# Key and query parts by batch, part and component in memory; a stack in two halves of eight heads

## The chip, the cores and the metric

The kernel runs on one core of one Trainium2 chip. The time is the device time in microseconds of one execution. The core has TensorE (PE, with its weight loads as PEld), VectorE (DVE), ScalarE (ACT), GpSimd (POOL) and SyncE (SP, here the queue that issues nearly all DMAs); 16 DMA engines move the data. Two per cent of the time is 9.9 us.

## What is computed

Two layers, each a cross-attention block and a mixture of experts, over x of shape (8, 128, 256). The first block is a long convolution of products of the context; the second, which the change concerns, is an attention with 16 heads of 8 components. Cut to that part:

```python
q = proj(Wq, bq, query).reshape(b, HD, H, n)          # b = 8, HD = 8, H = 16, n = 256
k = proj(Wk, bk, key).reshape(b, HD, H, n)            # key and value come from the context
q, k = (rotary(encoding, t) for t in (q, k))
scores = jnp.einsum('bdhn,bdhm->bhnm', q, k) / np.float32(np.sqrt(HD))
prob = jax.nn.softmax(scores, axis=-1)
x = jnp.einsum('bhnm,bdhm->bdhn', prob, v)
out = jnp.einsum('oi,bin->bon', Wm, x.reshape(b, d_model, n)) + bm[None, :, None]
...
x = x + jnp.tanh(g_xattn[1]) * _L1_xattn_ref(_layernorm(x, axis=-1), ctx_2048, ctx_2048, ...)
```

## The kernel before

The program is written out by hand, one instruction stream per engine, ordered by semaphores. It goes through the convolution (to about 84 us), the first experts (16 pairs of experts, to about 212 us, then the sum of their outputs in L1033 and L1038 to 282 us), the attention (about 258 to 410 us, its first row maxima between the expert sums), and the second experts (to the end). A pair of batches is a chunk `c`, of which there are four.

**Parts.** Keys and queries are float32; each is split into three bfloat16 parts. A product of two float32 numbers is the sum over part pairs, so a head's score is one matmul over 72 rows: 3 x 3 part pairs times 8 components. The rotated keys of a chunk are in `KR["a"]`, its parts in `KR["parts"]` (queries: `QR`); ACT casts parts 0 and 1 (`cast`, L591), POOL (keys, L430) or DVE (queries, L1309 to L1318) subtracts.

**Memory.** The layout must change: parts lie with component and head on partitions and position along the row, while a matmul needs components on partitions and one head at a time. So SP writes them to memory: keys at L316 during the convolution, once a chunk (`kp_out`), queries in `qout(c)` (L357, L358), once a chunk (`qp_out[c]`). Queries are written with five part rows, parts 0, 1, 2, 0, 1, so that three shifted windows can be read. Before ACT overwrites the parts of a chunk it waits for the write of the chunk before.

**Stacks.** `stack(b)` (L343) loads the key stack `KST[b % 4]` and the query stack `QST[b % 4]` of batch b, 72 rows of 16 heads times 256 positions each: for each of three groups of 24 rows one DMA for keys and one for queries, six in all, on one semaphore `st_in[b % 4]`. It waits until batch b - 4 has been used (`st_pe`), or until POOL has filled rows of ones (`kst_one`, L548). `maxrow(b)` (L351) adds three rows to the query stack with the negative row maxima.

**Order on PE.** `smax(H)` (L1007) multiplies the scores of head H (of 128 over all batches) for DVE's row maximum (`rowmax`, L1457); twenty of them run early, between the expert sums. In the attention loop group G = 8b + g computes `scores(G)` for two heads with the maximum rows (L1065, exponential on ACT, L708), `values` (L1080), and two more `smax` (three in the first four groups). At g = 4 stands `maxturn(b + 1)` (L1022), after the first `smax` of batch b + 2; DVE's `maxcopy` (L1478) then releases `maxrow(b + 1)` on SP. `smax` waits once a batch, at head 0, for the six DMAs of the stack.

**Order on SP** in this part: `qout(0)`, a wait for all key parts and query chunk 0, `stack(0)`, `stack(1)`, `qout(1)`, `qout(2)`, `maxrow(0)`, `stack(2)`; then for each b `maxrow(b + 1)`, `stack(b + 3)`, and for b = 0 `qout(3)`.

`P` = 128, `L` = 256, `NH` = 16, `HD` = 8, `NT` = 72, `UN` = 8, `NST` = 4, `QC` = 4, `B` = 8.

Of the kernel before, what the change touches and what calls it, by code (L numbers as in the profile page):

```python
# [22 lines left out]
BF16 = mybir.dt.bfloat16  # L23
# [6 lines left out]
B, S, L = 8, 128, 256  # L30
P = 128
# [20 lines left out]
TOP, LOW = B * HH * HD, B * HH * HH  # L52
HALF = TOP + LOW
NST = 4


def build(nc, x, ctx_in, g_xattn, g_ffn, ssm, dskip, gate_w, wgu, wdn, wsgu, wsdn, enc,
          wq, bq, wk, bk, wv, bv, wm, bm, rw, wa, wb, out):
    es = ExitStack()
    with es:  # L60
# [6 lines left out]

        kpad_d = nc.dram_tensor("kpad_d", [NH, P + L], F32, kind="Internal")
        rows_d = nc.dram_tensor("rows_d", [T + 1, L], F32, kind="Internal")
        kparts_d = nc.dram_tensor("kparts_d", [3, P, T * 2], BF16, kind="Internal")  # L70
        qparts_d = nc.dram_tensor("qparts_d", [5, P, T * 2], BF16, kind="Internal")


        X = sb("X", [P, B, L])
# [57 lines left out]
        OL = r2(14336, 2048, "p (k c) -> p k c", k=LB * B)  # L132

        def rope_views(base):
            return dict(a=base[:, 0:512], b=base[:, 512:1024],
                        parts=base[:, 1024:1792].bitcast(BF16).rearrange("p (s n) -> p s n", s=3))
        KR = rope_views(SA[:, :, :].rearrange("p s n -> p (s n)")[:, 0:1024 + 768])
        EB = SA[:, 2, 0:512].rearrange("p (k f c) -> p k f c", k=LB, f=2)

# [115 lines left out]
        mo_pe, mo_x = sem("mo_pe"), sem("mo_x")  # L255
        qp_pe, qp_free, qp_parts = sem("qp_pe"), sem("qp_free"), sem("qp_parts")
        qp_out = [sem(f"qp_out{c}") for c in range(B // 2)]
        st_in = [sem(f"st_in{s}") for s in range(NST)]
        kst_one = sem("kst_one")
        s_pe, s_max, ms_ok, mt_pe, mr_ok = (sem(n) for n in ("s_pe", "s_max", "ms_ok", "mt_pe", "mr_ok"))  # L260
        mrow_in, st_pe, p_ok, pv_pe = (sem(n) for n in ("mrow_in", "st_pe", "p_ok", "pv_pe"))
# [20 lines left out]
        @block.sync  # L282
        def _(sp):
            sp.dma_start(KPAD[:, P:P + L], ssm).then_inc(ld_ssm, 16)
            sp.dma_start(DSK[:, :], dskip.rearrange("(h a) -> h a", a=1)).then_inc(ld_ssm, 16)
            sp.dma_start(CTX[:, :, :], ctx_in.rearrange("b s l -> s b l")).then_inc(ld_ctx, 16)
            sp.dma_start(X[:, :, :], x.rearrange("b s l -> s b l")).then_inc(ld_x, 16)

            sp.wait_ge(kpad_ok, 1)
            sp.dma_start(kpad_d.ap(), KPAD).then_inc(kpad_out, 16)  # L290
            sp.wait_ge(kpad_out, 16)

            tap = bass.AP(tensor=kpad_d, offset=1, ap=[[1, P], [P + L, NH], [1, L]])
            sp.dma_start(TT, tap).then_inc(ld_tt, 16)
            sp.wait_ge(ld_w, 16 * 14)

            def load_up(k):
                sp.dma_start(WG[:, 2 * (k % NPAIR):2 * (k % NPAIR) + 2, :, :],
                             wgu[2 * k:2 * k + 2].rearrange("e (k p) f -> p e k f", p=P))\
                  .then_inc(ld_up[k % NPAIR], 16)  # L300

            def load_down(k):
                sp.dma_start(WD[0:HI, 2 * (k % NPAIR):2 * (k % NPAIR) + 2, :, :],
                             wdn[2 * k:2 * k + 2].rearrange("e (k p) n -> p e k n", p=HI))\
                  .then_inc(ld_down[k % NPAIR], 16)

            for k in range(NPAIR):
                load_up(k)
                load_down(k)
            sp.dma_start(SHW[:, :, :], wsgu.rearrange("(k p) f -> p k f", p=P)).then_inc(ld_sh, 16)  # L310
            sp.dma_start(SHD[:, 0:2, :], wsdn[0:256, :].rearrange("(k p) n -> p k n", p=P)).then_inc(ld_sh, 16)
            sp.dma_start(SHD[0:96, 2, :], wsdn[256:352, :]).then_inc(ld_sh, 16)

            for c in range(QC):
                sp.wait_ge(kp_parts, c + 1)
                sp.dma_start(kparts_d.ap().rearrange("s p n -> p s n")[:, :, c * 512:c * 512 + 512],  # L316
                             KR["parts"]).then_inc(kp_out, 16)

            sp.wait_ge(ln_ok, LN3)
            sp.dma_start(rows_d.ap()[1:T + 1, :].rearrange("(b s) l -> s b l", b=B), XN[:, :, :])\  # L320
              .then_inc(rows_out, 16)

            for k in range(NPAIR, KT0 + 1):
                if k < KT0:
                    sp.wait_ge(gu_pe, k - NPAIR + 1)
                    load_up(k)
                if k > NPAIR:
                    sp.wait_ge(y_pe, k - NPAIR)
                    load_down(k - 1)

            sp.wait_ge(y_pe, KT0)
            sp.dma_start(WA, wa.rearrange("e (k p) r -> p e k r", p=P)).then_inc(ld_ab, 16)
            sp.dma_start(WB, wb.rearrange("e p n -> p e n")).then_inc(ld_ab, 16)
            def stack(b):

                if b >= NST:
                    sp.wait_ge(st_pe, UN * (b - NST + 1))
                else:
                    sp.wait_ge(kst_one, b + 1)
                for r in range(3):  # L340
                    rows = slice(3 * HD * r, 3 * HD * r + 3 * HD)
                    for dst, src, part in ((KST, kparts_d, 0), (QST, qparts_d, r)):
                        sp.dma_start(dst[b % NST][rows, :, :],  # L343
                                     src.ap()[part:part + 3].rearrange("s (d h) (b n) -> (s d) h b n", h=NH, b=B)[:, :, b, :])\
                          .then_inc(st_in[b % NST], 16)

            def maxrow(b):

                sp.wait_ge(mr_ok, b + 1)
                for s in range(3):  # L350
                    sp.dma_start(QST[b % NST][NT + s:NT + s + 1, :, :].rearrange("p h (m n) -> p (h m) n", m=LB),  # L351
                                 MR[32 * s:32 * s + 32, :]).then_inc(mrow_in, 16)

            def qout(c):
                sp.wait_ge(qp_parts, c + 1)
                cols = slice(c * 512, c * 512 + 512)
                sp.dma_start(qparts_d.ap().rearrange("s p n -> p s n")[:, 0:3, cols], QR["parts"]).then_inc(qp_out[c], 16)  # L357
                sp.dma_start(qparts_d.ap().rearrange("s p n -> p s n")[:, 3:5, cols], QR["parts"][:, 0:2, :])\  # L358
                  .then_inc(qp_out[c], 16)

            qout(0)
            sp.wait_ge(kp_out, 16 * QC)
            sp.wait_ge(qp_out[0], 32)
            stack(0)
            stack(1)
            qout(1)
            qout(2)
            maxrow(0)
            sp.wait_ge(qp_out[1], 32)
            stack(2)  # L370
            for b in range(B):
                if b + 1 < B:
                    maxrow(b + 1)
                if b + 3 < B:
                    sp.wait_ge(qp_out[(b + 3) // 2], 32)
                    stack(b + 3)
                if b == 0:
                    qout(QC - 1)

            for c in range(2):  # L380
                sp.wait_ge(o_ok, 2 * c + 2)
                sp.dma_start(out.rearrange("b s l -> s b l")[:, 4 * c:4 * c + 4, :], X[:, 4 * c:4 * c + 4, :])\
                  .then_inc(out_dma, 16)
            sp.wait_ge(out_dma, 32)
            sp.wait_ge(zrow_out, 16)
# [3 lines left out]
        def _(pool):  # L389
# [93 lines left out]
                root(2 * c, 2 * c + 2)  # L483


            pool.wait_ge(kp_out, 16 * QC)
            def shared(u):
                n2, f = divmod(u, 3)
                m = SHF[f][1]
# [73 lines left out]
        def _(act):  # L563
# [19 lines left out]
            def cast(parts, a, c, s, q):  # L583

                if c >= 1 and s == 0:
                    act.wait_ge(qp_out[c - 1] if q else kp_out, 32 if q else 16 * c)
                if q:
                    act.wait_ge(cast_in, 2 * c + s + 1)
                else:
                    act.wait_ge(k_rest if s else k_sum, c + 1)  # L590
                act.activation(parts[:, s, :], a, ACT.Copy).then_inc(cast_out, 1)  # L591
# [193 lines left out]
        def _(pe):  # L785
# [211 lines left out]
            def smax(H):  # L997

                b, h = divmod(H, NH)
                if H == 0:  # L1000
                    pe.wait_ge(qp_free, 2)
                if h == 0:
                    pe.wait_ge(st_in[b % NST], 16 * 6 * (b // NST + 1))
                if H >= 2:
                    pe.wait_ge(s_max, H - 1)
                for m in range(LB):
# [231 lines left out]
        def _(dve):  # L1238
# [55 lines left out]
            def rope(c, R, bias, sem_pe, sem_free, sem_parts, cast0, b0):  # L1294

                def turn_up():
                    dve.wait_ge(sem_pe, c + 1)
                    if c >= 1:
                        dve.wait_ge(sem_parts, c)
                    dve.scalar_tensor_tensor(out=two(R["a"]), in0=two(PS[:, b0, :]), scalar=BT[:, bias:bias + 1],  # L1300
                                             in1=bc(FQ[:, 0, :], [P, 2, L], 1), op0=ALU.add, op1=ALU.mult)
                    dve.scalar_tensor_tensor(out=two(R["b"]), in0=two(PS[:, b0 + 1, :]),
                                             scalar=BT[:, bias + 1:bias + 2],
                                             in1=bc(FQ[:, 1, :], [P, 2, L], 1), op0=ALU.add, op1=ALU.mult)\
                        .then_inc(sem_free, 1)
# [218 lines left out]
            def qlast(i):  # L1524

                dve.wait_ge(qp_pe, QC + i)
                if i == 0:
                    dve.wait_ge(qp_parts, QC - 1)
                dve.scalar_tensor_tensor(out=two(QR["b" if i else "a"]), in0=two(PS[:, 7, :]),
                                         scalar=BT[:, 2 + i:3 + i], in1=bc(FQ[:, i, :], [P, 2, L], 1),  # L1530
                                         op0=ALU.add, op1=ALU.mult).then_inc(qp_free, 1)

# [135 lines left out]
```

## Time and profile before

| | |
|---|---|
| median of 3 runs | 494.24 us (487.6, 494.24, 494.79) |
| profiled execution | 491.66 us, span 489.8 us |
| granted TensorE clock, mean | 0.927 |
| PE, DVE, ACT, POOL busy | 84%, 60%, 34%, 31% of the span |

In the profile, times are microseconds from the start of the span unless marked ns. `SPq` is SP's queue: the duration of a row there is the time to issue a DMA, not to move it. A landing is when the DMA's semaphore is complete. PEclk is the share of full TensorE speed that was granted. The DMA share is the mean busy share of the 16 DMA engines. A name such as `R` can stand for several tiles of the same memory region; `kparts_d` and `qparts_d` are the tensors in memory. In brackets behind a row stands how long the engine was idle before it and what ended that.

### The profile page before, as it was taken

The page shows a single profiled execution, that of the slowest core. Times are in us where ns is not written, and L with a number is a line of the kernel's source. Part 1 is how long each engine was busy: PE and PEld are TensorE (multiplying, and loading weights), DVE is VectorE, ACT ScalarE, POOL GpSimd, SP SyncE. Part 2 cuts the span into 40 slices and gives each one's busy share as a digit, 9 for nine tenths or more (in the row PEclk, how much of TensorE's full clock was granted, in tenths as well). Part 3 has the DMA queues.
Part 4 walks back from the last instruction along what each step waited for, and adds up shares of the span by engine and source line. Part 5 has one row for each costly group of instructions (what it writes and reads, how often), then busy time and mean ns, then how long its engine had stood idle before and what let it go on. Part 6 is the DMA issues. An engine that isn't in the chain of part 4 may idle for free.

```text
span 489.8 us, 7462 instructions
## 1 busy us (share of the span) xinstructions
PE 413.6 (84%) x2821; PEld 266.0 (54%) x2821; DVE 295.0 (60%) x613; ACT 166.6 (34%) x300; POOL 153.8 (31%) x234
## 2 busy tenths in 40 slices
PE   1489993869769768699998768999999989899996
PEld 1378883824535435368886534455555545465554
DVE  1859997499916454633447778688898823322212
ACT  1221320133345434200110125467767785311110
POOL 0658898248972210502111060022112231110000
PEclk9999996588859998999999869699999999899999
DMA  6692010200049999741183141543345000000101
GB/s 197 190 286 87 33 34 32 87 0 0 1 121 267 254 258 233 188 143 36 58 162 83 57 97 34 119 87 75 64 78 98 3 3 1 1 0 1 43 0 43
DMA packets 49867, 43.53 MB, mean 89 GB/s; under 512 B 4101, under 2 KB 48553, under 8 KB 49833
## 3 DMA queue, kind: packets, MB, share of 16 engines
q1 hardware_dynamic: 47264, 40.65, 32.8%
q0 software_dynamic: 800, 2.10, 1.5%
q10 hardware_dynamic: 1768, 0.33, 0.4%
q8 instruction: 22, 0.36, 0.3%
q14 instruction: 13, 0.10, 0.1%
HBM read 36.55 MB, written 6.32 MB: 88 GB/s over the span
## 4 chain that ended last, share of the span: by engine, by line
PE 50%; DMA 16%; POOL 13%; DVE 11%; issue 3%; SPq 3%; ACT 3%; DVEq 0%; POOLq 0%; ACTq 0%
DMA WG<-in_L_ffn_w_gate_up_dram 10%; PE PS L1038 8%; PE PS L1221 7%; PE PS L1184 6%; PE PS L1080 5%; PE PS L1007 5%; PE PS L1065 4%; PE PS L957 3%; DMA R<-qparts_d 3%; DMA X<-in_x_dram 2%; DVE MX L1457 2%; PE PS L1033 2%; POOL SA L430 2%; POOL R L491 2%; SPq L343 2%
## 5 line engine op out<-in xcount | busy, mean ns | idle before, releaser
L1457 DVE TENSOR_REDUCE MX<-PS 128x2 f32<-128x512 f32 x128 | 85.9, 709 | 18.4 <-PE PS L1007 18.0
L708 ACT ACTIVATE R<-PS 128x1024 f32<-128x1024 f32 x64 | 65.4, 1024 | 46.9 <-PE PS L1065 46.5
L1038 PE MATMUL PS<-R 128*128 128x256 bf16 x384 | 47.3, 276 | 0.0
L1007 PE MATMUL PS<-R 72*128 72x256 bf16 x192 | 39.9, 295 | 6.6 <-DVE MX L1457 5.5
L1080 PE MATMUL PS<-R 128*32 128x256 f32 x512 | 42.6, 407 | 1.4 <-ACT R L718 1.0
L1038 PEld LDWEIGHTS PS<-R 128*128 128x128 bf16 x384 | 37.9, 99 | 5.9
L411 POOL TENSOR_TENSOR RSB<-RSA,MH 128x2 f32<-128x2 f32 (+2 forms) x20 | 14.3, 713 | 75.9 <-issue 40.2
L553 POOL TENSOR_TENSOR X<-X,R 128x256 f32<-128x256 f32 x8 | 5.8, 727 | 99.9 <-ACT R L731 99.9
L957 PE MATMUL PS<-WG,R 128*64 128x352 f32 x128 | 24.0, 496 | 14.8 <-DMA WG<-in_L_ffn_w_gate_up_dram 14.2
L1221 PE MATMUL PS<-WG,R 128*128 128x256 f32 x128 | 33.1, 405 | 1.3 <-DVE R L1624 1.2
L1065 PE MATMUL PS<-R 75*128 75x256 bf16 x192 | 31.6, 290 | 1.7 <-DMA R<-MR 1.7
L1624 DVE TENSOR_TENSOR R<-PS,R 128x512 f32<-128x512 f32 x16 | 11.0, 690 | 35.5 <-ACT R L775 35.5
L1007 PEld LDWEIGHTS PS<-R 72*128 72x128 bf16 x192 | 15.0, 103 | 29.0 <-DVE MX L1457 16.4
L1184 PE MATMUL PS<-CTX,WG 128*128 128x512 f32 x64 | 30.3, 595 | 0.0
L1221 PEld LDWEIGHTS PS<-WG,R 128*128 128x128 f32 x128 | 24.2, 198 | 7.7 <-issue 2.9
L518 POOL DMA_INDIRECT R<-rows_d,IX x16 | 15.4, 962 | 32.2 <-PE PS L947 30.4
L591 ACT ACTIVATE WD<-WD 128x512 bf16<-128x512 f32 x8 | 5.0, 628 | 58.9 <-DVE WD L1309 56.6
L1267 DVE TENSOR_SCALAR XN<-X,MV,RS 128x256 f32<-128x256 f32 x32 | 15.7, 525 | 14.8 <-POOL RS L415 14.8
L775 ACT ACTIVATE R<-PS 128x512 f32<-128x512 f32 x16 | 9.4, 597 | 43.1 <-PE PS L1197 39.8
L904 PE MATMUL PS<-CTX,SHW 128*128 128x512 f32 (+1 forms) x48 | 23.9, 661 | 0.0
L1065 PEld LDWEIGHTS PS<-R 75*128 75x128 bf16 x192 | 19.5, 104 | 7.7 <-DMA R<-MR 2.4
L957 PEld LDWEIGHTS PS<-WG,R 128*64 128x64 f32 x128 | 9.4, 145 | 25.7 <-issue 21.7
(237 smaller groups left out, 796.2 us busy)
## 6 DMA issues: line engine op xcount, KB each, us to landing
WG<-in_L_ffn_w_gate_up_dram SPq DMA_DIRECT2D x16, 704.0 KB, 12.6
WD<-in_L_ffn_w_down_dram SPq DMA_DIRECT2D x16, 352.0 KB
R<-kparts_d SPq DMA_DIRECT2D x24, 192.0 KB
R<-qparts_d SPq DMA_DIRECT2D x18, 192.0 KB
R<-kpad_d SPq DMA_DIRECT2D x1, 2048.0 KB, 7.9
kparts_d<-SA SPq DMA_DIRECT2D x4, 384.0 KB, 2.5
qparts_d<-WD SPq DMA_DIRECT2D x4, 384.0 KB, 3.2
SA<-qparts_d SPq DMA_DIRECT2D x6, 192.0 KB
```

The source lines that it names most:

```text
L518: pool.indirect_dma_start(XG[:, k % 4, :], None, rows_d.ap(), bass.IndirectOffsetOnAxis(ap=IX[:, k:k + 1], axis=0))\
L708: act.activation(PX[:, G % 4].rearrange("p h m n -> p (h m n)"), PS[:, 2 * (G % 2):2 * (G % 2) + 2, :].rearrange("p a n -> p (a n)"), ACT. ...
L904: last = pe.matmul(PS[0:m, 2 + 2 * (u % 2) + half, :], SHW[:, k, half * SH + f0:half * SH + f0 + m], XNT[:, k, n2 * 512:n2 * 512 + 512], s ...
L957: last = pe.matmul(PS[eo * SLOTC:eo * SLOTC + SLOTC, 2 + k % 2, 0:2 * INTER], XB[:, k % 2, j, eo * SLOTC:eo * SLOTC + SLOTC], WG[:, (2 * k ...
L1007: last = pe.matmul(PS[:, 4 + H % 2, m * L:m * L + L], QST[b % NST][0:NT, h, m * P:m * P + P], KST[b % NST][0:NT, h, :], start=True, stop=True)
L1038: last = pe.matmul(o, OHT[:, k, b * P:b * P + P], Y[:, k, s, :], start=False, stop=(k == KT0 - 1 and s == 2))
L1065: last = pe.matmul(PS[:, 2 * (G % 2) + hh, m * L:m * L + L], KST[b % NST][0:SROWS, 2 * g + hh, m * P:m * P + P], QST[b % NST][0:SROWS, 2 * ...
L1080: last = pe.matmul(PS[32 * j:32 * j + 32, 6, 0:L], V32[:, b % 2, m, 4 * q + j, :], PX[:, (2 * Q + j // 2) % 4, j % 2, m, :], start=(m == 0 ...
L1184: last = pe.matmul(PS[:, 4 + u % 2, :], WA[:, e, k, :], XNT[:, k, c * 512:c * 512 + 512], start=(k == 0), stop=(k == 1))
L1221: last = pe.matmul(PS[:, 2 * c + t // 2, (t % 2) * L:(t % 2) * L + L], AE[:, u % 2, t * P:t * P + P], WB[:, e, :], start=(e == 0 and t % 2 ...
L1267: ins = dve.tensor_scalar(XN[:, b, :], X[:, b, :], MV[:, b, 0:1], RS[:, b:b + 1], ALU.subtract, ALU.mult)
L1457: dve.tensor_reduce(MX[:, H % NH, :], PS[:, 4 + H % 2, :].rearrange("p (m n) -> p m n", m=LB), AX, ALU.max).then_inc(s_max, 1)
```

## The change

The tensors in memory are laid out by batch, part, component and head: `[B, 5, P, L]` for keys and `[B, 3, P, L]` for queries, so that one batch's part and component is a run of 16 heads times 256 positions (8 KB). The five part rows are now the keys', and the queries have three; the set of part pairs is the same. In SBUF the parts of a chunk are laid out by batch first. Keys of a chunk are written by four DMAs, queries by one. A stack is loaded by four DMAs (keys and queries, each in two halves of eight heads) of 72 rows of 4 KB each, whose source pattern has three leading entries: for keys with a step of one part, for queries with step 0. Each half has a semaphore, and `smax` waits for it at heads 0 and 8. DVE's rotary instructions take views of the same elements.

```diff
-        kparts_d = nc.dram_tensor("kparts_d", [3, P, T * 2], BF16, kind="Internal")
-        qparts_d = nc.dram_tensor("qparts_d", [5, P, T * 2], BF16, kind="Internal")
+        kparts_d = nc.dram_tensor("kparts_d", [B, 5, P, L], BF16, kind="Internal")
+        qparts_d = nc.dram_tensor("qparts_d", [B, 3, P, L], BF16, kind="Internal")
...
         def rope_views(base):
-            return dict(a=base[:, 0:512], b=base[:, 512:1024],
-                        parts=base[:, 1024:1792].bitcast(BF16).rearrange("p (s n) -> p s n", s=3))
+            flat = base[:, 1024:1792].bitcast(BF16)
+            return dict(a=base[:, 0:512].rearrange("p (b n) -> p b n", b=2),
+                        b=base[:, 512:1024].rearrange("p (b n) -> p b n", b=2),
+                        parts=flat.rearrange("p (b s n) -> p s b n", b=2, s=3),
+                        rows=flat.rearrange("p (r n) -> p r n", n=L))
...
-        st_in = [sem(f"st_in{s}") for s in range(NST)]
+        st_in = [[sem(f"st_in{f}_{s}") for s in range(NST)] for f in range(2)]
...
                 sp.wait_ge(kp_parts, c + 1)
-                sp.dma_start(kparts_d.ap().rearrange("s p n -> p s n")[:, :, c * 512:c * 512 + 512],
-                             KR["parts"]).then_inc(kp_out, 16)
+                for i in range(2):
+                    to = kparts_d.ap()[2 * c + i].rearrange("s p n -> p s n")
+                    sp.dma_start(to[:, 0:3, :], KR["rows"][:, 3 * i:3 * i + 3, :]).then_inc(kp_out, 16)
+                    sp.dma_start(to[:, 3:5, :], KR["rows"][:, 3 * i:3 * i + 2, :]).then_inc(kp_out, 16)
...
-                for r in range(3):
-                    rows = slice(3 * HD * r, 3 * HD * r + 3 * HD)
-                    for dst, src, part in ((KST, kparts_d, 0), (QST, qparts_d, r)):
-                        sp.dma_start(dst[b % NST][rows, :, :],
-                                     src.ap()[part:part + 3].rearrange("s (d h) (b n) -> (s d) h b n", h=NH, b=B)[:, :, b, :])\
-                          .then_inc(st_in[b % NST], 16)
+                for dst, src, parts, step in ((KST, kparts_d, 5, HD * ROW), (QST, qparts_d, 3, 0)):
+                    for f in range(2):
+                        rows = bass.AP(tensor=src, offset=b * parts * HD * ROW + f * (ROW // 2),
+                                       ap=[[step, 3], [ROW, 3 * HD], [1, ROW // 2]])
+                        sp.dma_start(dst[b % NST][0:NT, f * UN:f * UN + UN, :].rearrange("p h n -> p (h n)"), rows)\
+                          .then_inc(st_in[f][b % NST], 16)
...
             def qout(c):
                 sp.wait_ge(qp_parts, c + 1)
-                cols = slice(c * 512, c * 512 + 512)
-                sp.dma_start(qparts_d.ap().rearrange("s p n -> p s n")[:, 0:3, cols], QR["parts"]).then_inc(qp_out[c], 16)
-                sp.dma_start(qparts_d.ap().rearrange("s p n -> p s n")[:, 3:5, cols], QR["parts"][:, 0:2, :])\
+                sp.dma_start(qparts_d.ap()[2 * c:2 * c + 2].rearrange("b s p n -> p (b s) n"), QR["rows"])\
                   .then_inc(qp_out[c], 16)
...
-                if h == 0:
-                    pe.wait_ge(st_in[b % NST], 16 * 6 * (b // NST + 1))
+                if h % UN == 0:
+                    pe.wait_ge(st_in[h // UN][b % NST], 16 * 2 * (b // NST + 1))
```

`ROW` is `NH * L` = 4096 elements. The waits on `kp_out` count 64 a chunk and those on `qp_out[c]` count 16, as many as the DMAs now give.

## Rows read from the trace of the kernel before

**Rows 1.** The page: busy time, the 40 slices, the DMA queues.
```profile
PE 413.6 (84%) x2821; PEld 266.0 (54%) x2821; DVE 295.0 (60%) x613; ACT 166.6 (34%) x300; POOL 153.8 (31%) x234
...
q0 software_dynamic: 800, 2.10, 1.5%
```

**Rows 2.** The chain that ended last, in one turn of the batches: start, us, what.
```profile
322.44 0.84 SPq L343
...
326.61 6.31 DMA R<-qparts_d
```

**Rows 3.** Timeline of SP's queue: start us, us to issue, line, transfer.
```profile
242.94 0.93 SPq L343 DMA_DIRECT2D R<-kparts_d  x1
...
254.43 1.25 SPq L357 DMA_DIRECT2D qparts_d<-WD  x1
...
284.31 0.83 SPq L343 DMA_DIRECT2D R<-kparts_d  x1
...
302.41 0.83 SPq L343 DMA_DIRECT2D R<-kparts_d  x1
...
335.13 1.82 SPq L351 DMA_DIRECT2D SA<-MR  x3
337.06 0.82 SPq L343 DMA_DIRECT2D R<-kparts_d  x1
```

**Rows 4.** Timeline of PE: first score matmuls of batches 0, 2, 3, 4 and 7.
```profile
258.72 0.38 PE L1007 MATMUL PS<-R 72*128 72x256 bf16 x2
...
297.13 0.38 PE L1007 MATMUL PS<-R 72*128 72x256 bf16 x2
...
317.37 0.38 PE L1007 MATMUL PS<-R,SA 72*128 72x256 bf16 x2
...
332.96 0.39 PE L1007 MATMUL PS<-R 72*128 72x256 bf16 x2 [0.80 <-DMA R<-qparts_d]
...
376.56 0.38 PE L1007 MATMUL PS<-R,SA 72*128 72x256 bf16 x2
```

**Rows 5.** Busy time by stretch: us, then PE, PEld, DVE, ACT, POOL, PEclk, DMA share, GB/s.
```profile
284.00:298.00 14.00, 10.69 (x60) 4.58 (x58) 10.66 (x21) 4.12 (x5) 5.21 (x7) 0.63 0.44 85
298.00:318.00 20.00, 18.46 (x141) 9.27 (x137) 13.88 (x29) 10.20 (x15) 0.00 (x0) 0.74 0.42 94
...
333.00:347.00 14.00, 14.00 (x141) 8.17 (x142) 11.94 (x25) 9.99 (x17) 2.57 (x8) 1.00 0.44 87
...
362.30:376.50 14.20, 14.20 (x143) 8.27 (x144) 12.54 (x29) 10.61 (x17) 2.56 (x8) 1.00 0.44 86
```

**Rows 6.** The stack's line L343: who waited for it (us, times).
```profile
  PE PS L1007: 1.0, 2
```

**Rows 7.** Busy time by stretch, columns as in Rows 5: DMA share and GB/s last.
```profile
44.00:46.20 2.20, 2.20 (x13) 1.81 (x12) 2.17 (x4) 0.00 (x0) 2.20 (x5) 1.00 0.54 182
276.00:278.50 2.50, 1.81 (x15) 1.50 (x16) 1.94 (x6) 0.00 (x0) 0.00 (x0) 0.88 0.82 269
...
357.00:361.00 4.00, 4.00 (x46) 2.33 (x39) 3.78 (x8) 2.70 (x4) 0.36 (x2) 1.00 0.92 150
150.00:200.00 50.00, 38.60 (x307) 22.29 (x303) 25.64 (x66) 21.64 (x44) 8.21 (x9) 0.97 0.97 251
```

**Rows 8.** DMA issues: queue, count, KB each, median us to landing.
```profile
kparts_d<-SA SPq DMA_DIRECT2D x4, 384.0 KB, 2.5
...
R<-MR SPq DMA_DIRECT2D x18, 8.0 KB, 1.9
```

**Rows 9.** Timeline: ACT's cast that waits for qout(1), and head 16.
```profile
272.41 0.63 ACT L591 ACTIVATE WD<-WD 128x512 bf16<-128x512 f32 x1 [18.73 <-DVE WD L1309]
...
277.44 0.38 PE L1007 MATMUL PS<-R 72*128 72x256 bf16 x2
```

**Rows 10.** Timeline: key chunk 0 goes out, and the cast behind it.
```profile
43.59 0.37 SPq L316 DMA_DIRECT2D kparts_d<-SA  x1
...
49.63 0.63 ACT L591 ACTIVATE SA<-SA 128x512 bf16<-128x512 f32 x1 [8.09 <-POOL SA L424]
```

More of the change, by code:

```diff
@@ L54 @@
 NST = 4
+ROW = NH * L
 def build(nc, x, ctx_in, g_xattn, g_ffn, ssm, dskip, gate_w, wgu, wdn, wsgu, wsdn, enc,
@@ L355, in qout @@
                 sp.wait_ge(qp_parts, c + 1)
-                cols = slice(c * 512, c * 512 + 512)
-                sp.dma_start(qparts_d.ap().rearrange("s p n -> p s n")[:, 0:3, cols], QR["parts"]).then_inc(qp_out[c], 16)
-                sp.dma_start(qparts_d.ap().rearrange("s p n -> p s n")[:, 3:5, cols], QR["parts"][:, 0:2, :])\
+                sp.dma_start(qparts_d.ap()[2 * c:2 * c + 2].rearrange("b s p n -> p (b s) n"), QR["rows"])\
                   .then_inc(qp_out[c], 16)
             qout(0)
-            sp.wait_ge(kp_out, 16 * QC)
-            sp.wait_ge(qp_out[0], 32)
+            sp.wait_ge(kp_out, 64 * QC)
+            sp.wait_ge(qp_out[0], 16)
             stack(0)
@@ L368, in _ @@
             maxrow(0)
-            sp.wait_ge(qp_out[1], 32)
+            sp.wait_ge(qp_out[1], 16)
             stack(2)
@@ L374, in _ @@
                 if b + 3 < B:
-                    sp.wait_ge(qp_out[(b + 3) // 2], 32)
+                    sp.wait_ge(qp_out[(b + 3) // 2], 16)
                     stack(b + 3)
@@ L483, in _ @@
                 root(2 * c, 2 * c + 2)
-            pool.wait_ge(kp_out, 16 * QC)
+            pool.wait_ge(kp_out, 64 * QC)
             def shared(u):
@@ L585, in cast @@
                 if c >= 1 and s == 0:
-                    act.wait_ge(qp_out[c - 1] if q else kp_out, 32 if q else 16 * c)
+                    act.wait_ge(qp_out[c - 1] if q else kp_out, 16 if q else 64 * c)
                 if q:
@@ L1299, in turn_up @@
                         dve.wait_ge(sem_parts, c)
-                    dve.scalar_tensor_tensor(out=two(R["a"]), in0=two(PS[:, b0, :]), scalar=BT[:, bias:bias + 1],
+                    dve.scalar_tensor_tensor(out=R["a"], in0=two(PS[:, b0, :]), scalar=BT[:, bias:bias + 1],
                                              in1=bc(FQ[:, 0, :], [P, 2, L], 1), op0=ALU.add, op1=ALU.mult)
-                    dve.scalar_tensor_tensor(out=two(R["b"]), in0=two(PS[:, b0 + 1, :]),
+                    dve.scalar_tensor_tensor(out=R["b"], in0=two(PS[:, b0 + 1, :]),
                                              scalar=BT[:, bias + 1:bias + 2],
@@ L1528, in qlast @@
                     dve.wait_ge(qp_parts, QC - 1)
-                dve.scalar_tensor_tensor(out=two(QR["b" if i else "a"]), in0=two(PS[:, 7, :]),
+                dve.scalar_tensor_tensor(out=QR["b" if i else "a"], in0=two(PS[:, 7, :]),
                                          scalar=BT[:, 2 + i:3 + i], in1=bc(FQ[:, i, :], [P, 2, L], 1),
```

## The prediction

> **What bounds the kernel now.** I read the page's busy shares first: PE is busy 84% of the span, the next engine 60%, so PE and what it waits for set the time [rows 1]. The change touches only how key and query parts go to memory and come back, so I then followed the stretch where this matters, 243 to 377 us. The chain of waits passes in it twice through SP's queue and a stack's transfers: six issues of about 0.8 us, then 6.31 us to landing [rows 2], then PE's score matmul L1007. The SP queue shows why [rows 3]. In a steady batch one stack is issued from 322.44; PE's first L1007 on it runs at 332.96, after 0.8 us idle on the transfer [rows 4]; the maximum rows go out at 335.13 and the next stack at 337.06. These steps are a loop: on PE the transposition L1022 (which maxrow needs) stands behind the first L1007 of the next stack, and stack(b+3) stands behind maxrow(b+1) on SP. One turn is 10.5 us of stack (322.44 to 332.96) and 4.1 us of the rest (332.96 to 337.06), 14.6 in all. PE's own work on a batch is as long: the first L1007 of batches 4 and 7 are at 332.96 and 376.56, 14.53 us a batch [rows 4], with PE busy all of 14.00 and of 14.20 us in two of the three stretches between [rows 5]. So the stack's transfer has no slack. Anything that makes the first half of a stack land later than 10.5 us after its issue adds nearly all of that to each batch from 4 on; anything that makes it land sooner gains almost nothing, since PE becomes the only bound: PE waits 1.0 us in all for these transfers [rows 6].
>
> **The change, part by part.** *Fewer, longer pieces.* A stack is six DMAs of 24 rows in 512-byte pieces now: 6 x 192 KB = 1.18 MB. It becomes four DMAs of 72 rows of 4 KB. SP saves two issues of 0.8 us a stack, but the issues are not what is late: SP starts the last at 326.61 and the landing comes 6.31 us after [rows 2].
>
> *How the new DMAs are dealt out.* This decides the forecast. The source is now a pattern with three leading entries (step HD*ROW for keys, 0 for queries), 24 rows, and a run of 2048 elements. Neither step continues the 24 rows, so the leading count stays 3; all patterns before led with 24 rows or a whole tile of partitions. I take it that a transfer is dealt to the DMA engines by its leading entries, so that only three engines carry each of the four DMAs, and the same three each time. No row of before has a transfer with a leading count that small, so this is a premise that I choose because the pattern offers just three equal shares; its other end is no restriction at all (first rival). The Trainium skill, DMA: Bandwidth & Descriptors, section Rules for kernel authors, states it directly: an outermost dimension of c < 16, "e.g. a leading zero-stride broadcast of c copies", confines the whole DMA to at most c engines. By that rule queries and keys both get three engines; without it the change would be harmless. No trace here shows it yet.
>
> *What one engine carries.* Rate over (16 x share) gives GB/s of a busy engine [rows 7]: parts of 1 KB written undisturbed 182/(16 x 0.54) = 21.1; query parts 269/(16 x 0.82) = 20.5; expert weights in a full queue 251/(16 x 0.97) = 16.2; stacks in 512-byte pieces 150/(16 x 0.92) = 10.2. The software queue's 2.10 MB in 1.5% of the span [rows 1] make 17.9. Longer pieces go faster, and three engines do not crowd memory, so I go a little past the best row: 25 GB/s, an estimate, with 17.9 as the low end. A stack is 1.18 MB / 3 = 393 KB an engine: 15.7 us at 25, 18.6 at 21.1, 22.0 at 17.9. The skill's page, section Specifications, gives about 27 GiB/s an engine, which would make it 13.6 us.
>
> *First half.* PE now waits at heads 0 and 8 for a half each. The issue order is keys 0, keys 1, queries 0, queries 1, so the first half is complete only after three quarters of the bytes: 11.8 us, and about 2.0 us of latency (the transfer of 8 KB from MR takes 1.9, [rows 8]): 13.8 us in place of 10.5. The second half lands 3.9 us later and is wanted four groups (7.3 us) later: no cost. A loop is then 13.8 + 4.1 = 17.9 us, and the three engines are free again before the next stack (2.0 + 15.7).
>
> *Sum, with the positions of the profiled execution* [rows 2, 3, 4, 9]:
> Stacks 0 and 1 are issued from 242.9. The first half of stack 0 lands at 256.7, before its use at 258.72; stack 1's at 272.4, before head 16 (277.44). Cost 0. But queries of chunk 1 (qout(1), issued 254.4) lead with 128 partitions and use the three engines too, and there stand behind both stacks: 242.9 + 1.3 + 31.4 = 275.6 (of the 2.0 of latency I put 1.3 ahead of the bytes and 0.7 behind), their own share of 24 KB at 20.5 GB/s 1.2, landing 0.7: 277.6. ACT's cast of the next chunk waits for that and ran at 272.41; DVE's next step is right behind the cast, its row maxima behind that, and PE's L1007 behind these. **+5.2 us.**
> Stack 2 needs the two POOL fills after PE's last expert sum; issued 284.31 + 5.2 = 289.5, landed 303.3, wanted at 297.13 + 5.2 = 302.3: **+1.0**. Stack 3: issued 302.41 + 6.2 = 308.6, landed 322.4, wanted 317.37 + 6.2 = 323.6: 0; this long gap is a stretch of clock 0.74 [rows 5]. Stack 4: issued 322.44 + 6.2 = 328.6, landed 342.4, against 332.96 + 6.2 = 339.2: **+3.3**. Stacks 5, 6 and 7: 17.9 instead of 14.53, 3 x 3.4 = **+10.1**. After stack 7 nothing is loaded and the tail is the same. Together +19.6 us.
>
> *The key parts.* Each chunk goes out in four DMAs of 512-byte pieces (640 KB) instead of one of 384 KB. Chunk 1 (issue 43.59): three more issues of 0.4 bring the last to 44.8, landing 2.5 us later, or 4.2 if it grows with the bytes [rows 8]: 47.3 to 49.0. ACT's next cast, which waits for it, runs at 49.63 behind POOL's sum [rows 10]. POOL's chain hides it: 0; without that cover it would be at most 1.5 us a chunk, three times. *Queries out*: one DMA of 384 KB for two of 640 KB; the first is before stack(0) and may bring it 0.3 us forward: 0, and no more than 0.5 gained. *DVE's changed views* have the same elements: 0. *Splitting the semaphore*: no work; its gain is only that PE may start before the last DMA, which is in the numbers above.
>
> The profiled execution took 491.66 us (span 489.8), 2.6 under the median of the runs. 491.7 + 19.6 = 511.3; set against the median it would be 513.8. I give 512.
>
> **Rivals.**
> A, ends not slower: the four DMAs are spread widely, as those of before. At the 269 GB/s of [rows 7], 1.18 MB take 4.4 us, on three quarters of the engines 5.8; the first half lands 6.4 us after issue. The loop falls to 10.5, well under PE's 14.5, so the DMA leaves the chain and only PE's waits on it go: 1.0 us, and little more behind them. About 490 us. For it: the longer pieces are real, and stacks in 512-byte pieces run at half the rate of 1 KB ones. Against it: the leading count. It decides wherever the first half lands in under 10.5 us. Faster by over 2% would also need the low clock at 284 to 318 (0.63 and 0.74, [rows 5]) to lift.
> B, three engines at the low end, 17.9 GB/s: 22.0 us a stack, first half 18.5, loop 22.6. qout(1) lands at 290.1: +17.7; stack 2 +5.7, stack 3 +3.5, stack 4 +8.0, three loops +24.3: +59, 551 us. For it: it is the one rate of [rows 1] for a queue by itself; against: that queue ran beside full weight loads.
> C, three engines, but the loss under 2% because only the loops count and an engine moves nearly 29 GB/s: 13.6 us a stack, loop 16.3, stack 4 +1.7, three times 1.8: about 500.
> Idle PE may also be granted less clock: in 284 to 298, busy 10.69 of 14 us, it was 0.63 [rows 5]. In the loops PE's idle time absorbs part of that; up to 10 us on top of the forecast, in its own range.
>
> **Chances.** Forecast 0.64 (502 to 525 us), A 0.20 (of it 0.05 faster by over 2%), B 0.12, C 0.04. Two per cent, 9.9 us, is about what a measurement tells from no change. Faster 0.05, same 0.19, slower 0.76. The range 489 to 535 takes in A's centre and stops short of B.
>
> **What would show it.** Right: the four transfers of a stack (KB 288 each) land 17 us after the first issue, the DMA share in a stack's stretch is about 0.19 (3 of 16) at 70 to 80 GB/s, PE idles 3 us at the first L1007 of each batch on the queries' transfer, turns are near 18 us, and ACT's cast near 272 comes 5 us late. Wrong: a share over 0.5 with 200 GB/s, first halves in 7 us, PE without such idle time. If the share is low but the cast near 272 is on time, the term of qout(1) was wrong.

## The result, and the profile after

The changed kernel is slower: 524.76 us, median of 4 runs (521.66 to 530.04), against 490.92 (482.79 to 494.79) for the kernel before, now with a fourth run. The ratio is 1.079 with a 95% interval of 1.058 to 1.101. I had forecast 512, in 489 to 535. The direction and the mechanism were right; the loss is 34 us by the medians where 18 to 20 were forecast. The profiled execution took 530.04 us with a span of 528.1, the longest of the four and 38 us longer than the profiled one of before, so its positions serve to place the loss and not to measure it. Every ratio here is formed from the fast executions of both kernels, the medians from all.

The page of the changed kernel: PE's busy share, the DMA queues (packets, MB, share of the 16 engines) and the stack's transfers.

```profile
PE 434.6 (82%) x2821; PEld 273.6 (52%) x2821; DVE 295.8 (56%) x613; ACT 167.5 (32%) x300; POOL 153.5 (29%) x234
...
DMA packets 37482, 43.53 MB, mean 82 GB/s; under 512 B 3748, under 2 KB 33864, under 8 KB 37448
...
R<-kparts_d SPq DMA_DIRECT2D x16, 288.0 KB
R<-qparts_d SPq DMA_DIRECT2D x12, 288.0 KB
```

The bytes are as many as before, in longer pieces, and PE is busy 21 us longer with the same 2821 matmuls [rows 1]. The mean granted clock fell with it, from 0.927 to 0.884; the clock comes back below. In this kernel the stack's DMAs stand in L350 (L343 of before), the maximum rows in L357 (L351), the query parts in L362, PE's score matmuls in L1011 (L1007). First the transfers, by stretch (us, then PE, PEld, DVE, ACT, POOL busy, PEclk, DMA share, GB/s):

```profile
357.00:368.00 11.00, 7.05 (x71) 4.02 (x70) 7.52 (x20) 5.82 (x9) 1.32 (x5) 0.99 0.19 78
```

Here only a stack is moved. The share is 0.19, that is 3.04 engines of 16, and 78 / 3.04 = 25.7 GB/s an engine; I had written "about 0.19 (3 of 16)" and 25. The stacks of before moved 150 GB/s on twelve engines (counted in the first experiment), 12.5 GB/s each, so an engine now moves twice as much, and there are a quarter as many: a whole stack lands 18.0 us after its first issue, where it took 10.5. SP's queue and PE at one such stack (timeline):

```profile
353.80 1.53 SPq L350 DMA_DIRECT2D R<-kparts_d  x2
355.38 1.41 SPq L350 DMA_DIRECT2D R<-qparts_d  x2
371.13 1.82 SPq L357 DMA_DIRECT2D R<-MR  x3
373.06 1.53 SPq L350 DMA_DIRECT2D R<-kparts_d  x2
```
```profile
368.09 0.61 PE L1011 MATMUL PS<-R 72*128 72x256 bf16 x2 [4.03 <-DMA R<-qparts_d]
```

The first half is there 14.3 us after the first issue (before, the whole stack was there after 10.5, [rows 2, 3]); PE, idle for 4.03 us, takes up batch 5 at once; the maximum rows go out 3.0 us later and the next stack 1.9 after that. All over the run, who waited for the stack's line: the 1.0 us of [rows 6] became 14.7.

```profile
  PE PS L1011: 14.7, 5
```

The second loss is at the query chunk. The chain of waits from 259 to 281 us, and ACT's cast (272.41 in [rows 9]):

```profile
257.12 3.55 SPq L350
...
260.71 18.28 DMA qparts_d<-WD
```
```profile
279.02 0.63 ACT L595 ACTIVATE WD<-WD 128x512 bf16<-128x512 f32 x1 [23.76 <-DMA qparts_d<-WD]
```

The cast is 6.6 us later than before. Not all of that is the chunk's: the first score matmul of batch 0 (258.72 in [rows 4]) was 1.6 us late already. The first of batch 1 stands behind the cast; before (first row) and after:

```profile
274.51 0.38 PE L1007 MATMUL PS<-R 72*128 72x256 bf16 x2 [0.23 <-DVE MX L1457]
...
260.29 0.38 PE L1011 MATMUL PS<-R 72*128 72x256 bf16 x2
...
281.12 0.59 PE L1011 MATMUL PS<-R 72*128 72x256 bf16 x2 [5.22 <-DVE MX L1461]
```

The step from batch 0 to batch 1 grew from 15.8 to 20.8 us, by 5.0.

The third I had set at nothing. Two stretches of the changed kernel with PE busy without a gap:

```profile
326.00:347.40 21.40, 21.40 (x123) 10.59 (x123) 11.25 (x21) 8.23 (x11) 2.56 (x8) 0.52 0.19 70
...
406.50:429.00 22.50, 22.46 (x123) 11.08 (x124) 11.34 (x21) 9.01 (x14) 2.55 (x8) 0.50 0.04 13
```

At 0.50 TensorE runs at the lower of its two levels, 1.2 GHz, and 123 matmuls are recorded in 21.4 us, where a stretch of 14.20 us at full clock holds 143 [rows 5]. Just ahead of both PE had stood idle for the stack, 3.91 us to 325.92 and 4.20 us to 406.54.

Put together by the first score matmul of a batch in both profiled executions:

| stretch | before | after | loss, us |
|---|---|---|---|
| start to batch 2 | 297.1 | 306.8 | 9.7 |
| batch 2 to 3 | 20.2 (clock 0.75) | 19.1 (1.00) | -1.1 |
| batch 3 to 4 | 15.6 (1.00) | 23.3 (0.56) | 7.7 |
| batch 4 to 7 | 14.3, 14.9, 14.3 | 18.8, 19.8, 18.7 (0.99, 0.75, 0.97) | 13.7 |
| batch 7 to the end | 113.2 (0.98) | 121.6 (0.91) | 8.4 |

The sum is 38.4 us, the 38.3 between the spans but for rounding.

### The profile page after: what moved, and what is told of

Its sections match the earlier page's. It is cut to its first block, busy times and chain, and to the rows that moved or that the text cites. A ratio compares the mean times of both kernels' runs of the same rounds, so it can differ in the third digit from the quotient of the medians.

```text
span 528.1 us, 7462 instructions
## 1 busy us (share of the span) xinstructions
PE 434.6 (82%) x2821; PEld 273.6 (52%) x2821; DVE 295.8 (56%) x613; ACT 167.5 (32%) x300; POOL 153.5 (29%) x234
## 4 chain that ended last, share of the span: by engine, by line
PE 38%; DMA 29%; POOL 12%; DVE 8%; SPq 6%; issue 3%; ACT 3%; DVEq 0%; POOLq 0%; ACTq 0%
DMA WG<-in_L_ffn_w_gate_up_dram 10%; DMA R<-qparts_d 7%; PE PS L1225 6%; PE PS L1188 5%; DMA SA<-qparts_d 5%; SPq L350 4%; PE PS L1084 4%; DMA qparts_d<-WD 4%; PE PS L1042 4%; PE PS L1011 3%; PE PS L1069 3%; PE PS L961 3%; DMA X<-in_x_dram 2%; POOL SA L434 2%; POOL R L495 2%
## 5 line engine op out<-in xcount | busy, mean ns | idle before, releaser
L1011 PE MATMUL PS<-R 72*128 72x256 bf16 x192 | 40.3, 297 | 17.5 <-DVE MX L1461 10.8
L1084 PE MATMUL PS<-R 128*32 128x256 f32 x512 | 48.4, 457 | 1.4 <-ACT R L722 1.0
L1042 PEld LDWEIGHTS PS<-R 128*128 128x128 bf16 x384 | 38.4, 100 | 6.3
L961 PE MATMUL PS<-WG,R 128*64 128x352 f32 x128 | 26.3, 535 | 13.7 <-DMA WG<-in_L_ffn_w_gate_up_dram 13.1
L1069 PE MATMUL PS<-R 75*128 75x256 bf16 x192 | 36.5, 324 | 1.0 <-DMA R<-MR 1.0
L1011 PEld LDWEIGHTS PS<-R 72*128 72x128 bf16 x192 | 15.0, 103 | 40.2 <-DVE MX L1461 15.9
L1225 PE MATMUL PS<-WG,R 128*128 128x256 f32 x128 | 31.6, 391 | 1.3 <-DVE R L1628 1.2
L1225 PEld LDWEIGHTS PS<-WG,R 128*128 128x128 f32 x128 | 23.1, 189 | 7.3 <-issue 2.9
L1069 PEld LDWEIGHTS PS<-R 75*128 75x128 bf16 x192 | 22.0, 117 | 8.8 <-issue 2.3
L1011 PE MATMUL PS<-R,SA 72*128 72x256 bf16 x64 | 18.8, 393 | 8.1 <-DMA SA<-qparts_d 8.1
L1271 DVE TENSOR_SCALAR XN<-X,MV,RS 128x256 f32<-128x256 f32 x32 | 15.7, 525 | 14.7 <-POOL RS L419 14.7
L908 PE MATMUL PS<-CTX,SHW 128*128 128x512 f32 (+1 forms) x48 | 23.3, 645 | 0.0
L779 ACT ACTIVATE R<-PS 128x512 f32<-128x512 f32 x16 | 9.4, 596 | 41.7 <-PE PS L1201 38.3
```

Source lines behind the costliest of these rows:

```text
L908: last = pe.matmul(PS[0:m, 2 + 2 * (u % 2) + half, :], SHW[:, k, half * SH + f0:half * SH + f0 + m], XNT[:, k, n2 * 512:n2 * 512 + 512], s ...
L961: last = pe.matmul(PS[eo * SLOTC:eo * SLOTC + SLOTC, 2 + k % 2, 0:2 * INTER], XB[:, k % 2, j, eo * SLOTC:eo * SLOTC + SLOTC], WG[:, (2 * k ...
L1011: last = pe.matmul(PS[:, 4 + H % 2, m * L:m * L + L], QST[b % NST][0:NT, h, m * P:m * P + P], KST[b % NST][0:NT, h, :], start=True, stop=True)
L1042: last = pe.matmul(o, OHT[:, k, b * P:b * P + P], Y[:, k, s, :], start=False, stop=(k == KT0 - 1 and s == 2))
L1069: last = pe.matmul(PS[:, 2 * (G % 2) + hh, m * L:m * L + L], KST[b % NST][0:SROWS, 2 * g + hh, m * P:m * P + P], QST[b % NST][0:SROWS, 2 * ...
L1084: last = pe.matmul(PS[32 * j:32 * j + 32, 6, 0:L], V32[:, b % 2, m, 4 * q + j, :], PX[:, (2 * Q + j // 2) % 4, j % 2, m, :], start=(m == 0 ...
```

## The experiments

They set four causes against each other: the three engines (by the leading count), the pieces themselves, the order of the transfers, and the clock. Each ratio is against the kernel before, run on the same chip beside it. A step is the time from the first score matmul of one batch to that of the next.

**One. The order of the two outer counts alone.**

```diff
-                                       ap=[[step, 3], [ROW, 3 * HD], [1, ROW // 2]])
+                                       ap=[[ROW, 3 * HD], [step, 3], [1, ROW // 2]])
```

> Only the order of the two outer counts of the stack's source changes, from 3 x 24 to 24 x 3, for keys and queries alike (the 72 rows of both stacks come in another, common order). Theory 1, a transfer is dealt to the engines by its leading count: 12 engines instead of 3 carry a stack, DMA share in a stack's stretch over 0.5 and not 0.19, the four transfers land some 7 us after the first issue and not 17, PE waits for no stack, and the time is that of the kernel before, 486 to 492 us. Rival, the 4 KB pieces or the 72 rows of one transfer are what is slow, however they are dealt: share and landing stay as in the changed kernel, about 522 us.

487.49 us, ratio 0.9945 (0.988 to 1.001): the whole loss is gone with one line. A stretch of its trace in which a stack is moved, and SP's queue:

```profile
319.00:323.00 4.00, 3.87 (x42) 1.80 (x42) 3.62 (x8) 3.23 (x5) 2.41 (x8) 1.00 0.67 173
```
```profile
317.54 2.01 SPq L350 DMA_DIRECT2D R<-kparts_d  x2
319.59 1.56 SPq L350 DMA_DIRECT2D R<-qparts_d  x2
330.24 1.83 SPq L357 DMA_DIRECT2D SA<-MR  x3
332.17 1.67 SPq L350 DMA_DIRECT2D R<-kparts_d  x2
```

The share is 0.67, over three times that of three engines, and one turn takes 14.63 us. Nobody waited for line 350, and from batch 3 each batch takes 14.6 us at full clock. A stack's first half lands 8.0 us after the first issue and the last transfer 9.0, a little over the 7 expected. The pieces, the number of rows and the bytes are the changed kernel's, so the pieces are not what is slow. The leading count decides how many engines carry a transfer, which had been a premise. The semaphore events that the trace keeps count them: besides one near the issue, a transfer's semaphore gets three events at its end in the changed kernel (360.40, 360.45 and 360.52 us), twelve in this run (321.48 to 321.82 for the first transfer), and twelve also in the kernel before. By the Trainium skill, DMA: Bandwidth & Descriptors, section Rules for kernel authors, an outermost dimension of fewer than 16 confines a DMA to at most so many engines; the traces agree, 0.19 with a leading 3. The Trainium skill's same page, section Why a DMA increments its semaphore by 16 and not by 1, gives the largest count up to 16 that divides both outermost sizes, so 12 for 24 and 72; the twelve events agree. The shares alone would not settle that number: 0.67 here is under 12/16, but the stacks of before show 0.92 [rows 7]. The share adds up the times of packets, and these overlap on an engine: in that row up to 19 are under way at once.

The same 4 KB pieces moved 173 GB/s on twelve engines here, 14.4 each, against the 25.7 of three alone. So the 25.7 is not the length of the pieces alone: twelve engines at work together are each slower.

**Two. The halves in order**, three engines kept.

```diff
-                for dst, src, parts, step in (...):
-                    for f in range(2):
+                for f in range(2):
+                    for dst, src, parts, step in (...):
```

> The changed kernel with the four transfers issued keys 0, queries 0, keys 1, queries 1; still three leading entries. Theory, the loop from one stack's first half to the next issue costs most: the first half lands after 8 + 2 = 10 us instead of 14.4, the loop falls to some 14.5 us, but the three engines need 16 us for a stack, so a batch takes 16 to 17 instead of 19 to 20.6. The stop at the query chunk near 279 stays. Time 504 to 510 us. Rival, the lost time is that three engines cannot carry the bytes at all, whatever the order: within 4 us of the changed kernel, 518 to 526. Rival, it is the granted clock that falls after each long wait of PE: then the shorter waits let the clock stay at 1.00 and the time falls under 504.

506.97 us, ratio 1.038 (1.026 to 1.049). The same bytes on the same three engines cost 18 us less because the half that is wanted first goes first. Its steps from batch 2 on were 16.0, 23.0 (clock 0.68) and 18.5 us (0.75), and then:

```profile
362.00:377.60 15.60, 14.80 (x145) 8.24 (x144) 13.82 (x35) 11.51 (x18) 2.55 (x8) 1.00 0.19 68
377.60:393.20 15.60, 14.45 (x144) 8.54 (x145) 12.60 (x26) 10.18 (x17) 2.55 (x8) 1.00 0.20 79
```

The last two are 15.6 us, near the 16 I put as the engines' limit. The rival that the order does not matter falls. A new wait takes the old one's place: the maximum rows stand behind the second half on the three engines, and PE's L1069 waits 11.8 us in all for them.

```profile
  DMA R<-MR: 11.8, 9
```

Behind one of these waits, of 2.42 us, PE runs at the lower level for 23.5 us; the two slow steps are there:

```profile
329.73 1.03 PE L1069 MATMUL PS<-R 75*128 75x256 bf16 x4 [2.42 <-DMA R<-MR]
...
329.00:352.50 23.50, 22.77 (x125) 11.49 (x126) 11.61 (x24) 8.70 (x11) 1.17 (x5) 0.50 0.15 58
```

**Three. The query chunk between stacks 0 and 1.**

```diff
             stack(0)
-            stack(1)
             qout(1)
+            stack(1)
             qout(2)
```

> The changed kernel with the write of query chunk 1 issued between stacks 0 and 1 instead of behind both. Theory, the write stands behind both stacks on the three engines: it lands near 262 instead of 279, ACT's cast runs at 272 again, stack 1's first half still lands by 275 before it is used at 277, and the time falls by 6 to 7 us to 514 to 517. Rival, the stop is covered later (stack 2 waits anyway): under 2 us gained. Rival, the stop also costs clock afterwards: 8 to 14 us gained, and the granted clock from 284 to 307 higher than 0.66.

518.23 us, ratio 1.060 (1.045 to 1.076), 6.5 us under the changed kernel's median. ACT's cast waits for DVE again, not for the chunk, and runs at 273.45:

```profile
273.45 0.63 ACT L595 ACTIVATE WD<-WD 128x512 bf16<-128x512 f32 x1 [18.78 <-DVE WD L1313]
```

The interval is wider than the effect, so the time alone would not do. The position does: the step from batch 0 to 1 is 15.9 us, where it was 20.8. The fifth run leaves this term alone.

**Four and five. Three engines for a part of the stacks.** The source pattern is chosen by batch, 24 leading for the others.

```diff
+                                       ap=([[step, 3], [ROW, 3 * HD], [1, ROW // 2]] if b >= 2 else
+                                           [[ROW, 3 * HD], [step, 3], [1, ROW // 2]]))
```

(in the fifth run `b < 2`).

> Leading count 3 for stacks 2 to 7 only; stacks 0 and 1 with 24. Theory, two terms that add up: this one holds the loops, 491 + (31 - 7) = 515 us, with stacks 2 to 7 moved at 75 GB/s, and the cast at 272. If the granted clock carries most of the excess over the forecast of 20 us, stretches of over 20 us at 0.5 to 0.6 follow a stack's wait here too, and without them a batch takes 18.5 us.

> The complement of the run with three leading entries for stacks 2 to 7: three for stacks 0 and 1 alone, 24 for the others. Theory, two terms: here the query chunk's write lands near 279 and ACT's cast is 6 to 7 us late, and the batches from 2 on take 14.6 us: 487.5 + 6.6 = 494 us. Rival, the first term is taken up by later slack: 488 to 490. Rival, the stop also costs clock: over 498.

Three engines for stacks 2 to 7: 513.24, 524.04, 524.44 and 529.56 us, median 524.24, too spread for an interval. The shortest is near the 515 forecast, the other three are the time of the whole change. For stacks 0 and 1 alone: 493.96 us, ratio 1.014 (1.008 to 1.019), as forecast; the cast is late and the batches from 3 on take 14.6 us:

```profile
278.53 0.63 ACT L596 ACTIVATE WD<-WD 128x512 bf16<-128x512 f32 x1 [23.76 <-DMA qparts_d<-WD]
```

The size of the first term is best read from the step between batches 0 and 1: 20.6 to 20.9 us in the four traces with the query chunk behind both stacks on three engines (the changed kernel, runs two, five and seven), 15.8 to 15.9 in the kernel before and in runs one, three, four, six, eight and ten. That is 5.0 us. The medians are coarser: the fifth run is 6.5 us above the first, but 4.0 above the sixth, which was measured beside it. Two steps of the fourth run's trace (of the execution of 524.44 us) suggest why stacks 2 to 7 alone can cost as much as the whole change:

```profile
362.20:381.20 19.00, 14.51 (x144) 8.39 (x145) 13.55 (x32) 11.34 (x18) 2.56 (x8) 0.96 0.18 67
381.20:405.60 24.40, 24.40 (x143) 12.31 (x144) 12.67 (x24) 10.33 (x16) 2.55 (x8) 0.54 0.16 59
```

The same work takes 19.0 us at a mean clock of 0.96, bound by the loop, and 24.4 at 0.54, bound by PE itself. An execution with one such step more would be some 5 us longer; that this is what spreads the four times is not shown, since only one of them has a trace.

**Six. Both cures**: leading 24 and the halves in order.

> Leading count 24 and the halves in order: keys 0, queries 0, keys 1, queries 1. Theory: with 12 engines a stack is there well before PE wants it, so an earlier first half changes nothing: 484 to 491 us, no difference from the run with the count alone. Rival, stack 3 or the maximum rows still profit: 2 to 4 us less.

489.97 us, ratio 1.006 (1.001 to 1.010). In its profile batches from 3 on take 14.6 us, as in the first run; with 24 leading the order gains nothing.

**Seven. PE kept busy ahead of the wait.**

```diff
+                if h == 0 and b >= 2:
+                    for _ in range(48):
+                        pe.matmul(PS[:, 4 + H % 2, 0:P], ONB[:, :], UPB[:, :], start=True, stop=True)
                 if h % UN == 0:
                     pe.wait_ge(st_in[h // UN][b % NST], 16 * 2 * (b // NST + 1))
```

(the wait for `s_max` stands ahead of the added matmuls.)

> The changed kernel with 48 extra matmuls of 128 columns on PE ahead of the wait for each stack from 2 on (into a PSUM bank that the next score matmul overwrites, so the result is not touched): 48 x 0.057 = 2.7 us at full clock, 5.1 at half. Theory, on top of the transfer's own loop the time is lost to low clock after PE's idle waits: filled, the waits no longer lower the clock, batches 3 to 7 all take 18.5 to 19 us at 0.95 or more, the tail starts at full clock, and the time falls by 6 to 14 us to 510 to 518 although work was added. Rival, the low-clock stretches do not come from the waits: the extra matmuls lengthen the batches at low clock, 525 to 540 us.

524.0 us, ratio 1.075 (1.067 to 1.083): no different from the changed kernel, so neither number came in. The trace, from batch 2 to 7:

```profile
307.50:326.60 19.10, 16.83 (x187) 10.28 (x186) 13.62 (x28) 10.10 (x14) 0.00 (x0) 1.00 0.23 81
326.60:345.10 18.50, 17.04 (x190) 10.92 (x191) 13.14 (x29) 10.23 (x14) 2.57 (x8) 1.00 0.19 71
345.10:363.50 18.40, 17.17 (x192) 11.13 (x193) 13.13 (x29) 10.79 (x17) 2.56 (x8) 1.00 0.18 67
363.50:382.50 19.00, 17.15 (x192) 11.12 (x192) 13.13 (x29) 10.79 (x17) 2.55 (x8) 1.00 0.18 67
382.50:408.80 26.30, 26.30 (x192) 14.89 (x193) 13.84 (x29) 11.33 (x17) 2.55 (x8) 0.61 0.15 55
```

Four batches in a row at full clock, which the changed kernel does not have; what is left of PE's waits for a stack is at most 2.1 us. From batch 2 on one stretch at the lower level is left, where the changed kernel's trace has three. That fits a link from wait to clock. But the fifth step fell to 0.61 after an idle wait of only 1.85 us, and with the added matmuls in it that step takes 26.3 us. By positions, the steps from batch 2 to 7 take 101.3 us against the changed kernel's 99.7, and the tail behind batch 7 takes 111.4 us at full clock against 121.6 at 0.91. In the times nothing is left of this, so the run does not show what the clock costs in a typical execution.

**Eight. Both orders**, three engines kept.

> Three leading entries as in the changed kernel, with both orders changed: halves in order and query chunk 1 between stacks 0 and 1. Theory, the terms add: start stop gone (6.5 us), loop at the 16 us that three engines need for a stack: 496 to 503 us, batches at 15.6 to 16.5 us. Rival, without the count nothing below the run with the halves in order is to be had: 504 to 510.

502.19 us, ratio 1.023 (1.012 to 1.035): the terms add, in the forecast's range. Steps from batch 2 on are 15.0 to 16.0 us at full clock; 18.7 and 21.4 at 0.82 and 0.76.

**Nine. PE waits for both halves at head 0.**

> The changed kernel, but PE waits for both halves of a stack at head 0. Theory, every microsecond by which what PE waits for lands later is paid once a batch: the last transfer lands some 4 us behind the third, so the steps between first score matmuls grow from 18.7 to about 22.5 us at full clock, over stacks 2 to 7, and the time grows by 16 to 24 us to 541 to 549. Rival, the three engines' 16 us a stack are the limit and not the loop: steps and time stay, 520 to 530 us.

554.66 us, ratio 1.145 (1.134 to 1.156), 30 us above the changed kernel where I had put 16 to 24. The rival (no cost) falls. In the traces the five steps from batch 2 to 7 take 119.2 us against 99.7, 3.9 us more a batch, as the later landing would give; the traced executions are 24.0 us apart, and the changed kernel's is 5.3 above its median. Steps from batch 2 on are 22.7 to 24.4 us, and the waits up to 8.5 us, with clock 0.50 to 0.54 in every second step. This is also what the two semaphores of the change are worth with three engines.

**Ten. The first run again**, more rounds.

> The run with the counts 24 x 3 once more, with more rounds, beside the kernel before: does the layout with pieces of 4 KB, once 12 engines carry it, beat the kernel before? Theory: PE's steps of 14.6 us are the bound in both, and the gain is the stretch of stacks 3 and 4, 0 to 4 us, under 1 per cent. Rival: it is worth 4 to 8 us.

489.92 us, ratio 0.996 (0.989 to 1.003). Together with the first run (0.9945) and the sixth (1.006): the new layout with 24 leading makes no difference that these runs can tell. The step from batch 2 to 3 is shorter in their traces (15.3 to 15.7 us at full clock for 20.2 at 0.75), as the expectation had it, but the times do not show it. There is no version here that beats the kernel before.

## Why the prediction was right, and where it fell short

- *Three engines by the leading count*: right (share 0.19 and three events a transfer; 0.67 and twelve in the first run with only the count changed).
- *25 GB/s an engine*: 25.7. No row of mine was above 21.1, and those figures divided by the share, which counts overlapping packets (the stacks moved 12.5 an engine, not 10.2). That three engines alone would each be faster than any row was a guess, and its closeness is partly luck. The stack's first half lands 14.3 to 14.8 us after the issue, not 13.8, the rest of the turn takes 4.5, not 4.1, and a turn takes 18.7 to 18.8 us, not 17.9. The term of three loops, +10.1, measured +13.7, of it about 1 in the step at clock 0.75.
- *The query chunk*: +5.2 forecast, 5.0 measured by the step from batch 0 to 1. From the first issue of stack 0 (244.36) to the cast (279.02) are 34.7 us, as in my sum (242.9 to 277.6). The other 1.6 us of delay were there before batch 0; they are within what the traces scatter at this place (257.7 to 263.0 us, the ninth run aside).
- *Stack 2*: +1.0 forecast. Batch 2 is 9.7 us late, so 3.1 on top of the 6.6 of before: the POOL fill ended later, since PE's last expert sums ran at the lower level (284 to 292 at 0.67).
- *Stack 3*: 0 forecast. PE did wait 3.91 us here, because this stretch now ran at full clock; in the step that is -1.1.
- *Stack 4*: +3.3 forecast, +7.7 measured. The wait was not for the stack: PE was busy for all of 326.0 to 347.4 at 0.52.
- *Key parts, query parts, DVE's views*: 0, and the first run bears it out. It has all of them and the time of the kernel before.
- *The tail*: "After stack 7 nothing is loaded and the tail is the same". This is the step that failed. It is 8.4 us longer: the last stack's wait left PE at the lower level for 22.5 us.

So the mis-sized term is the clock. I had "up to 10 us on top of the forecast" for it, "in its own range", and added none of it to the number. From the rows: 4.5 us in the step of stack 4 (23.3 against 18.8), 1 in that of stack 6, 8.4 in the tail, some 1.5 at stack 2, about 15 us of 38 in this execution. That sum is an account of rows, not an experiment: the run that was to isolate it came out even. It holds for this execution alone: the other three were 2.3 to 8.4 us shorter, at mean clocks of 0.864 to 0.882, lower still than this one's 0.884. Shown is that idle waits stand just ahead of the stretches at 1.2 GHz, that one such stretch is left from batch 2 on where the waits are filled and three where not, and that the same step takes 19 or 24 us by clock. How long a wait must be is not shown. The kernel before has such a stretch too, after 1.18 us:

```profile
305.15 1.00 PE L1065 MATMUL PS<-R 75*128 75x256 bf16 x4 [1.18 <-DMA R<-MR]
...
305.20:315.50 10.30, 10.30 (x58) 5.21 (x58) 5.29 (x9) 3.46 (x4) 0.00 (x0) 0.50 0.72 157
```

Of the rivals, A was what the first run made of the change, 487 us for my 490, with its first half after 8.0 us and not 6.4. B and C fell with the 25.7 GB/s.

## What to carry to other kernels

Read a DMA's access pattern from its slowest count before anything else: a merged load led by a count of 3 ran on three engines, and exchanging two entries, free because both operands of the contraction are permuted alike, gave the loss back. Cost a wait on PE twice, once by its length and once by the clock that the following work is granted. Where transfers set the pace, issue first what is waited for first (18 us on three engines, nothing on twelve).

## What I had not expected of the hardware

- SP is held back by its own transfers. With three engines full, the timeline shows issues that take 0.7 us otherwise taking 3.55 each, so that the query chunk was issued at 260.71, where before it was at 254.43 [rows 3]:

```profile
247.48 6.01 SPq L350 DMA_DIRECT2D R<-kparts_d  x2
253.53 7.14 SPq L350 DMA_DIRECT2D R<-qparts_d  x2
260.71 3.52 SPq L362 DMA_DIRECT2D qparts_d<-WD  x1
```

  The late issue cost next to nothing. Of the sixteen landing events of the chunk's write thirteen came by 266.46 us and three from 278.41 to 278.99, just behind the last transfer of stack 1 (277.95): the write uses all sixteen engines and waited on the three that carried the stacks.

- The lower level stays for 20 us and more though PE is busy without a gap (21.40 of 21.40 us at 0.52), and in the seventh run it came after an idle wait of 1.85 us, while waits of 2.14 and 1.33 us earlier in the same run did not bring it.
